# Opening order of a quantised macaron block: first transfers, tables and down units reordered, and weight stores issued from another queue

## The chip, the cores and the metric

The kernel runs on one core of a Trainium2 chip. The metric is the device time of one execution in microseconds (us), lower is better. Times of before: 858.51, 859.09 and 859.96 us in three runs, median 859.09.

## The reference

The input is 2048 tokens of 512 float32 features (two sequences of 1024). Three stages follow each other, each on a layer norm of the running sum:

```python
x = x + 0.5 * ffn(layernorm(x))        # gate, up, down with 4-bit weights, 512 -> 1376 -> 512
x = x + attention(layernorm(x))        # one head of width 128
x = x + 0.5 * ffn(layernorm(x))        # the same weights again
# ffn: W[k,n] = scales[g_idx[k],n] * (w4[k,n] - (z4[g_idx[k],n] + 1)) for gate, up and down
#      h = silu(x @ Wg) * (x @ Wu);  out = h @ Wd
```

Eight 4-bit values are packed in an int32; scales and zeros come per group of 128 rows, and which group a row uses is itself an input (`g_idx`).

## The kernel before, in words

**Tiling.** The inner dimension of 1376 is cut into 11 tiles (`NT`), the last 96 wide. The 2048 tokens make four pairs of 512-row halves. "Pair 0" is the first 1024 rows of the first feed-forward stage; while it works on its top half (`plain_top`), the weights are dequantised tile by tile, split into a high and a low float32r part and kept for all later pairs. Every product is three passes (`PASSES`: high-high, high-low, low-high).

**Units.** Gate, up and down of one tile are three *units*: 33 in all. `unit(u)` (L334) gives `(u % 3, u // 3)`, so the order is gate 0, up 0, down 0, gate 1, and so on. One unit passes through these steps, each on its own engine:

1. SyncE's queue loads the packed values, each packed row eight times, in `load_units` (L484 to L503), into one of six slots: four issues for a gate or up unit, one for a down unit. From unit 6 on it waits until the unit that had the slot is unpacked.
2. VectorE shifts and masks (`unpack`, L1681).
3. TensorE multiplies a one-hot matrix by a table of zeros and one of scales (`scales_zeros`, L789; bf16, L811 for gate and up, L808 for down): these spread the groups over the rows, into PSUM banks 2 and 3. It waits for the unit before to be dequantised (`s_wf`).
4. VectorE subtracts the zeros and multiplies by the scales (`dequantise`, L1691; the product into `wf` is L1705). `wf` has two slots, so the product of unit u waits until the low part of unit u-2 is made and until the float32 store of unit u-2 has landed (`d_full`, L1704).
5. ScalarE copies `wf` to the high part (`w_hi`, L1255); GpSimd subtracts to get the low part (`w_lo`, L2096).
6. SyncE's queue stores the float32 values of gate and up units to `wfull` (`save_full`, L519, issue L523); a later phase reads them back.

**What sets the order.** All of it is written by hand: each engine has a program of its own, and semaphores join them. SyncE's queue is strictly in order: in the loop at L583, `save_full(u)` comes ahead of `load_units([u + 6])`, the row loads and the saves of finished tiles (`save_plain`, L514), so a store waits behind the issues ahead of it.

**The opening.** SyncE issues the gate and up scales, their zeros, the group numbers, identity and shifts, then unit 0 (L563 to L571). ScalarE's queue issues the four row tiles of x (256 KB each) and the gate and up group indices, GpSimd's the down scales, zeros and indices. GpSimd cuts each scale into three bf16 parts (`cut_scales`, five steps), VectorE unpacks the zeros (`unpack_zeros`), and `table` (L401) sends these to the table tiles: the up table by SyncE, the gate table by ScalarE, in both cases after all five cuts and the zeros. VectorE computes the layer-norm statistics (L1615 to L1625), GpSimd the power -0.5 (L2088), ScalarE applies it (L1245), TensorE transposes the rows (L1020). The one-hots take a clamp, a compare and a second compare (`clamp`, `compare_low`, `one_hot`): for gate and up on VectorE, for the 768 down columns on GpSimd with the last step on VectorE. `keep_warm(n)` (L732) issues n dummy matmuls of 128x128.

**TensorE's tile loop** (L815) is: gate product i, table products of a unit to come, up product i, table products, down product i-1, table products. It runs `keep_warm(6)` after up 0, and before the loop `keep_warm(10)`, `(6)`, `(6)`.

Of the kernel before, what the change touches and what calls it, by code (L numbers as in the profile page):

```python
# [7 lines left out]
F32 = mybir.dt.float32  # L8
# [64 lines left out]
def macaron(nc, x, w_qkv, b_qkv, w_o, b_o, packed, scales, zeros, g_idx, ident, shifts, groups, out):  # L73
    ctx = ExitStack()
    with ctx:
# [52 lines left out]
        spare = place("spare", [P, 1], F32)  # L128
        mx = place("mx", [P, QT], F32)
# [115 lines left out]
        def sem(name):  # L245
# [3 lines left out]
        d_small, d_grp, d_cut_gu, d_cut_d, d_idx_gu, d_idx_d, d_bqkv, d_wq, d_wo, d_bo = (  # L249
            sem(n) for n in ("d_small", "d_grp", "d_cut_gu", "d_cut_d", "d_idx_gu", "d_idx_d", "d_bqkv", "d_wq", "d_wo", "d_bo"))  # L250
# [82 lines left out]

        def unit(u):  # L334
            return u % 3, u // 3
# [17 lines left out]
        for n in range(UNITS):  # L353
            q_count[n % QSLOTS] += 16 * (1 if n % 3 == 2 else KT)
            q_ready.append(q_count[n % QSLOTS])
# [11 lines left out]
        def full_saves(u):  # L367

            return 16 * len([v for v in range(u % 2, u, 2) if v % 3 < 2])
# [31 lines left out]
        def table(eng, m, at_row=0):  # L401
# [6 lines left out]
            for j in range(3):  # L408
                eng.dma_start(dst[at_row + j * g:at_row + (j + 1) * g, :], parts[:, j, :]).then_inc(done, 16)
            row = at_row + Z_ROW  # L410
            eng.dma_start(dst[row:row + g, :], zb.rearrange("p c j -> p (c j)")).then_inc(done, 16)
# [39 lines left out]
        GU_COLS, DOWN_COLS = slice(0, HID), slice(HID, HID + D_COLS)  # L451

# [4 lines left out]
        def out_bank(b, j):  # L457
            return PT_BANK + j % 2 if by_dve(b, j) else OUT_BANK

# [3 lines left out]
        def _(sp):  # L463
# [20 lines left out]
            def load_units(units):  # L484
                for u in units:
                    if u >= UNITS:
                        return
                    m, i = unit(u)
                    s = u % QSLOTS
                    if u >= QSLOTS:  # L490

                        sp.wait_ge(s_int, u - QSLOTS + 1)
                    for k in range(1 if m == 2 else KT):

                        if m == 2:
                            rows = packed[2][i * 16:i * 16 + width(i) // PACK, :]
                            dst = qs[:, s, :, :].rearrange("p k c -> p (k c)")[0:width(i), :]
                        else:
                            rows = packed[m][k * 16:(k + 1) * 16, i * P:i * P + width(i)]
                            dst = qs[:, s, k, 0:width(i)]  # L500
                        n_rows, n_cols = rows.shape
                        src = rows.rearrange("r (o c) -> r o c", o=1).to_broadcast([n_rows, PACK, n_cols])
                        sp.dma_start(dst, src).then_inc(d_q[s], 16)  # L503

# [9 lines left out]
            def save_plain(i):  # L514
                sp.wait_ge(s_wlo, 3 * i + 2)
                sp.dma_start(kept(i, slice(P1, P2 + 1)), as_kept(i, plain(i)[:, 0:2, :, :, :])).then_inc(d_kept[i], 16)
                sp.dma_start(kept(i, slice(P3, P3 + 1)), as_kept(i, plain(i)[:, 3:4, :, :, :])).then_inc(d_kept[i], 16)

            def save_full(u):  # L519
                m, i = unit(u)  # L520
                if m < 2:
                    sp.wait_ge(s_wf, u + 1)
                    sp.dma_start(unit_view(u, wfull[i, :, m, :]), unit_view(u, wf[:, u % 2, :])).then_inc(d_full[u % 2], 16)  # L523
# [40 lines left out]
            for m in range(2):  # L564
                sp.dma_start(sc_gu[:, m * SC:(m + 1) * SC], flat(scales[m], SC)).then_inc(d_cut_gu, 16)
            for m in range(2):
                sp.dma_start(zq_gu[m * ZP:(m + 1) * ZP, :], flat(zeros[m], ZC)).then_inc(d_cut_gu, 16)
            sp.dma_start(grp[:, :], groups).then_inc(d_grp, 16)
            sp.dma_start(idt[:, :], ident).then_inc(d_small, 16)
            sp.dma_start(shift[:, :], shifts).then_inc(d_small, 16)  # L570
            load_units([0])  # L571

            sp.wait_ge(s_cut, CUT_STEPS)
            sp.wait_ge(s_tab, ZERO_STEPS)
            table(sp, 1)
            load_units([1, 2])
            sp.wait_ge(s_cut, 2 * CUT_STEPS)
            sp.wait_ge(s_tab, 2 * ZERO_STEPS)
            table(sp, 2)
            load_units([3, 4, 5])  # L580


            for u in range(UNITS):  # L583
                save_full(u)
                load_units([u + QSLOTS])
                if u == 3:
                    load_rows(1, x, ROWS)
# [4 lines left out]
                if u >= 4 and u % 3 == 1:  # L592
                    save_plain(u // 3 - 1)
# [49 lines left out]
            sp.dma_start(wo_raw[:, :], w_o).then_inc(d_wo, 16)  # L643
# [72 lines left out]
        def _(pe):  # L716
# [72 lines left out]
            def scales_zeros(u):  # L789
# [4 lines left out]
                w = width(i)  # L794
                if u:
                    if u in (2, 3 * D_TILES + 2):

                        if u == 2:
                            pe.wait_ge(s_oh, 4)
                        pe.wait_ge(d_tab[2 if u == 2 else 3], 64)  # L800

                    pe.wait_ge(s_wf, u)
                g = (GK, GK, GD)[m]
                row = FOLD if m == 1 or (m == 2 and i >= D_TILES) else 0
                for rows, bank in ((slice(row + Z_ROW, row + Z_ROW + g), Z_BANK), (slice(row, row + 3 * g), S_BANK)):
                    if m == 2:
                        col = i * P - (D_FROM if row else 0)
                        mm = pe.matmul(ps[0:w, bank, :], oh_d[rows, col:col + w], tab_d[rows, :], start=True, stop=True)  # L808
                    else:
                        for k in range(KT):  # L810
# [4 lines left out]
            def plain_top():  # L815

                for i in range(NT):
                    pe.wait_ge(s_wlo, 3 * i + 1)
# [3 lines left out]
                    if i == 0:  # L822

                        plain_product(0, 0, 0, by_tile=True)
                        scales_zeros(2)
# [1412 lines left out]
```

## Time and profile before

| what | us |
|---|---|
| median of three runs (lowest to highest) | 859.09 (858.51 to 859.96) |
| the profiled execution | 858.8 |
| its span, first to last instruction | 857.0 |
| TensorE busy in the span | 832.5 |
| VectorE / ScalarE / GpSimd busy | 479.6 / 271.1 / 243.1 |

PE is TensorE, PEld its weight loads, DVE VectorE, ACT ScalarE, POOL GpSimd, SP SyncE; a q behind a name is that engine's instruction queue, which also issues DMAs. Times in a timeline are from the span's start. A bracket behind a row says how long the engine was idle before it and whose event ended that. Matmuls are pipelined, so a busy TensorE is not TensorE at its peak, and dummy matmuls count as busy.

### The profile page before, as it was taken

The page shows a single profiled execution, that of the slowest core. Times are in us where ns is not written, and L with a number is a line of the kernel's source. Part 1 is how long each engine was busy: PE and PEld are TensorE (multiplying, and loading weights), DVE is VectorE, ACT ScalarE, POOL GpSimd, SP SyncE. Part 2 cuts the span into 40 slices and gives each one's busy share as a digit, 9 for nine tenths or more (in the row PEclk, how much of TensorE's full clock was granted, in tenths as well). Part 3 has the DMA queues.
Part 4 walks back from the last instruction along what each step waited for, and adds up shares of the span by engine and source line. Part 5 has one row for each costly group of instructions (what it writes and reads, how often), then busy time and mean ns, then how long its engine had stood idle before and what let it go on. Part 6 is the DMA issues. An engine that isn't in the chain of part 4 may idle for free.

```text
span 857.0 us, 10735 instructions
## 1 busy us (share of the span) xinstructions
PE 832.5 (97%) x4040; PEld 677.3 (79%) x4040; DVE 479.6 (56%) x800; ACT 271.1 (32%) x465; POOL 243.1 (28%) x197
## 2 busy tenths in 40 slices
PE   4799999999999999999999999999999999999998
PEld 4477678887888888788888888888887888888786
DVE  5577763564745463455877686545445744444452
ACT  3233222253511211242565783112212511112121
POOL 6344431463200524030225453151510201101100
PEclk9999999999999999999999999999999999999999
DMA  5667647895485444241215237844444064444121
GB/s 135 203 202 245 216 172 229 306 338 200 166 329 171 129 167 123 77 160 67 82 55 169 71 130 259 324 149 157 139 136 164 36 212 145 153 154 148 40 98 50
DMA packets 72271, 139.36 MB, mean 163 GB/s; under 512 B 25548, under 2 KB 36476, under 8 KB 67228
## 3 DMA queue, kind: packets, MB, share of 16 engines
q1 hardware_dynamic: 70908, 136.91, 47.5%
q10 hardware_dynamic: 1152, 1.36, 0.6%
q8 instruction: 32, 0.52, 0.3%
q0 software_dynamic: 160, 0.42, 0.2%
q14 instruction: 19, 0.16, 0.1%
HBM read 100.54 MB, written 37.95 MB: 162 GB/s over the span
## 4 chain that ended last, share of the span: by engine, by line
PE 73%; DVE 1%; ACT 1%; issue 0%; POOL 0%; DVEq 0%; ACTq 0%; POOLq 0%
PE ps L722 37%; PE ps L729 34%; PE ps L740 2%; PE ps L1125 1%; DVE pT L1604 0%; ACT pr L1464 0%; POOL t L2083 0%; ACT oT L1240 0%; PE ps L1051 0%; DVE oT L1604 0%; DVE t L1604 0%; DVE hT L1604 0%; DVE mx L1920 0%; ACT xn L1245 0%; DVE u L1607 0%
## 5 line engine op out<-in xcount | busy, mean ns | idle before, releaser
L722 PE MATMUL ps<-blk,ring 128*128 128x512 f32 (+1 forms) x1386 | 320.9, 389 | 0.1
L722 PEld LDWEIGHTS ps<-blk,ring 128*128 128x128 f32 (+1 forms) x1386 | 256.7, 185 | 58.1 <-DVE blk L1604 0.5
L729 PE MATMUL ps<-wd,hT 128*128 128x512 f32 (+1 forms) x1056 | 250.7, 392 | 0.8 <-DVE hT L1604 0.7
L729 PEld LDWEIGHTS ps<-wd,hT 128*128 128x128 f32 (+1 forms) x1056 | 196.8, 188 | 43.4 <-DVE hT L1604 1.2
L2125 POOL TENSOR_TENSOR h<-h,u 128x512 f32<-128x512 f32 (+1 forms) x33 | 42.7, 1295 | 324.2 <-ACT h L1359 324.2
L729 PE MATMUL ps<-xT,wp 128*128 128x512 f32 x480 | 115.7, 395 | 0.9 <-POOL wp L2083 0.7
L729 PEld LDWEIGHTS ps<-xT,wp 128*128 128x128 f32 x480 | 88.4, 188 | 22.4 <-issue 2.0
L1607 DVE TENSOR_TENSOR u<-ps,p1s 128x512 f32<-128x512 f32 (+1 forms) x66 | 45.4, 687 | 97.3 <-PE ps L722 97.2
L1359 ACT ACTIVATE h<-h 128x512 f32<-128x512 f32 (+1 forms) x33 | 20.9, 632 | 176.1 <-DVE h L1607 176.1
L1607 DVE TENSOR_TENSOR u<-ps,u 128x512 f32<-128x512 f32 (+1 forms) x66 | 45.6, 691 | 25.6 <-PE ps L722 24.6
L1607 DVE TENSOR_TENSOR h<-ps,p1s 128x512 f32<-128x512 f32 (+1 forms) x33 | 22.8, 691 | 64.1 <-PE ps L722 64.1
L1604 DVE TENSOR_TENSOR hT<-h,hT 128x512 fp32r<-128x512 f32 (+1 forms) x44 | 30.7, 712 | 24.8 <-ACT hT L1240 24.8
L1354 ACT ACTIVATE g<-ps 128x512 f32<-128x512 f32 (+1 forms) x33 | 19.7, 598 | 76.0 <-PE ps L722 76.0
L1240 ACT ACTIVATE hT<-u 128x512 fp32r<-128x512 f32 (+1 forms) x33 | 20.9, 632 | 64.5 <-DVE u L1811 64.5
L1811 DVE TENSOR_TENSOR u<-u,g 128x512 f32<-128x512 f32 (+1 forms) x33 | 38.8, 1177 | 1.1
L2093 POOL TENSOR_SCALAR xn<-xn,mv,rstd 128x512 f32<-128x512 f32 x18 | 38.3, 2139 | 0.5
L1240 ACT ACTIVATE hT<-h 128x512 fp32r<-128x512 f32 (+1 forms) x44 | 27.0, 629 | 35.5 <-PE ps L729 35.5
L2083 POOL TENSOR_TENSOR wp<-wf,wp 128x512 fp32r<-128x512 f32 x20 | 26.7, 1333 | 39.3 <-ACT wp L1240 39.3
L1604 DVE TENSOR_TENSOR hT<-u,hT 128x512 fp32r<-128x512 f32 (+1 forms) x33 | 22.8, 692 | 23.1 <-ACT hT L1240 23.1
L2088 POOL TENSOR_TENSOR rstd<-rstd,mhalf 128x4 f32<-128x4 f32 x12 | 14.9, 1244 | 69.5 <-DVE rstd L1625 69.5
L1836 DVE SCALAR_TENSOR_TENSOR xres<-ps,xres 128x512 f32<-128x512 f32 x32 | 21.6, 689 | 18.7 <-PE ps L729 18.5
L1604 DVE TENSOR_TENSOR wi<-qs,ps 128x512 bf16<-128x512 int32 (+2 forms) x33 | 22.3, 676 | 16.9 <-PE ps L811 12.0
(124 smaller groups left out, 877.7 us busy)
## 6 DMA issues: line engine op xcount, KB each, us to landing
ring<-wsaved SPq DMA_DIRECT2D x29, 1024.0 KB, 5.1
ring<-wsaved SPq DMA_DIRECT2D x33, 768.0 KB, 4.4
wsaved<-wp SPq DMA_DIRECT2D x10, 1024.0 KB, 4.5
stream<-xres SPq DMA_DIRECT2D x32, 256.0 KB, 2.3
xn<-stream SPq DMA_DIRECT2D x8, 1024.0 KB, 6.7
xres<-stream SPq DMA_DIRECT2D x32, 256.0 KB, 4.0
wfull<-wf SPq DMA_DIRECT2D x20, 256.0 KB, 2.8
wsaved<-wp SPq DMA_DIRECT2D x10, 512.0 KB, 3.0
```

The lines of the kernel that those rows point to most:

```text
L722: mm = pe.matmul(ps[0:w, bank, :], ring[:, slot, which, a, kt, 0:w], blk[:, which, b, kt, :], start=not onto and kt == 0 and n == 0, stop= ...
L729: mm = pe.matmul(bank_ap, lhs(a), rhs(b), start=first and n == 0, stop=last and n == 2)
L1240: return act.activation(dst, src, ACT.Copy)
L1354: act.activation(g1[0:w, n % 2, :], ps[0:w, product_bank(n // NT + 1, 0), :], ACT.Silu).then_inc(s_g1, 1)
L1359: act.activation(hidden(i)[0:width(i), :], hidden(i)[0:width(i), :], ACT.Silu).then_inc(s_g2, 1)
L1604: return dve.tensor_tensor(out=dst, in0=a, in1=b, op=ALU.subtract)
L1607: return dve.tensor_tensor(out=dst, in0=a, in1=b, op=ALU.add)
L1811: dve.tensor_tensor(out=u2[0:w, n % 2, :], in0=u2[0:w, n % 2, :], in1=g1[0:w, n % 2, :], op=ALU.mult)\
L1836: dve.scalar_tensor_tensor(out=xres[:, r, :], in0=ps[:, down_bank(q, half, r), :], scalar=0.5, in1=xres[:, r, :], op0=ALU.mult, op1=ALU.ad ...
L2083: return pool.tensor_tensor(out=dst, in0=a, in1=b, op=ALU.subtract)
L2093: pool.tensor_scalar(x_rows(t)[:, r, :], x_rows(t)[:, r, :], mv[:, t % 2, r, 0:1], rstd[:, t % 2, r:r + 1], ALU.subtract, ALU.mult).then_i ...
L2125: pool.tensor_tensor(out=hidden(i)[0:w, :], in0=hidden(i)[0:w, :], in1=u3[0:w, n % 2, :], op=ALU.mult).then_inc(s_h2, 1)
```

## The change

- **Unit order.** Gate 0, up 0, then for each tile gate i, up i, down i-1, and the last down at the end. `made(m, i)` gives a unit's place; waits that had `3 * i + n` use it.
- **First transfers.** On SyncE the group numbers move ahead of the zeros; the zeros get semaphores of their own (`d_zq_gu`, `d_zq_d`). ScalarE's queue takes the down zeros ahead of x, and units 0 and 1 after the indices. GpSimd's index loads move behind the first cut.
- **Tables.** SyncE sends all gate and up pieces, each as soon as it is cut; ScalarE sends none.
- **ScalarE** runs one Silu on a spare column early, and issues the float32 store of a gate or up unit itself, right behind its copy of it. It applies the layer norm of the second 512 rows, which VectorE did.
- **One-hots of down.** The first 128 columns are made first; GpSimd makes its part of the other 640 ahead of the low parts of units 3 and 4, VectorE its part in tile 1.
- **TensorE.** Table products of unit 0 come ahead of the row transposes, those of unit 1 between the second and third row tile, those of unit 2 ahead of gate 0. `keep_warm` is 4 and 4 ahead of the loop (10, 6, 6 before) and 2 after up 0 (6 before).
- Smaller: one semaphore for two attention weights instead of two, later places of `deviation(1)` and of the second rows' statistics.

```diff
+        UNIT_ORDER = ((0, 0), (1, 0)) + tuple(mi for i in range(1, NT) for mi in ((0, i), (1, i), (2, i - 1))) + ((2, NT - 1),)
         def unit(u):
-            return u % 3, u // 3
+            return UNIT_ORDER[u]
+        def made(m, i):
+            return UNIT_ORDER.index((m, i)) + 1
...
@@ sync
+            sp.dma_start(grp[:, :], groups).then_inc(d_grp, 16)
             for m in range(2):
-                sp.dma_start(zq_gu[...], flat(zeros[m], ZC)).then_inc(d_cut_gu, 16)
-            sp.dma_start(grp[:, :], groups).then_inc(d_grp, 16)
+                sp.dma_start(zq_gu[...], flat(zeros[m], ZC)).then_inc(d_zq_gu, 16)
...
-            load_units([0])
-            sp.wait_ge(s_cut, CUT_STEPS)
-            sp.wait_ge(s_tab, ZERO_STEPS)
-            table(sp, 1)
-            load_units([1, 2])
+            for j in range(3):
+                sp.wait_ge(s_cut, 2 * j + 1)
+                for m in range(2):
+                    table(sp, m, pieces=(j,))
+            sp.wait_ge(s_tab, 2 * ZERO_STEPS)
+            for m in range(2):
+                table(sp, m, pieces=(3,))
+            load_units(sp, [2, 3])
             sp.wait_ge(s_cut, 2 * CUT_STEPS)
-            sp.wait_ge(s_tab, 2 * ZERO_STEPS)
             table(sp, 2)
-            load_units([3, 4, 5])
+            load_units(sp, [4, 5])
             for u in range(UNITS):
-                save_full(u)
-                load_units([u + QSLOTS])
-                if u == 3:
+                load_units(sp, [u + QSLOTS])
+                if u == 5:
                     load_rows(1, x, ROWS)
...
@@ tensor, plain_top
                     plain_product(0, 0, 0, by_tile=True)
-                    scales_zeros(2)
...
                     scales_zeros(3)
                     plain_product(0, 0, 1, (2, 3))
-                    scales_zeros(4)
-                    keep_warm(6)
+                    keep_warm(2)
...
@@ tensor, opening
-            keep_warm(10)
+            keep_warm(4)
+            pe.wait_ge(d_tab[0], 64)
+            pe.wait_ge(s_oh, 3)
+            scales_zeros(0)
             for r in range(RT):
+                if r == 2:
+                    pe.wait_ge(d_tab[1], 64)
+                    scales_zeros(1)
                 pe.wait_ge(s_ln[0], r + 1)
...
-            scales_zeros(0)
-            keep_warm(6)
-            pe.wait_ge(d_tab[1], 64)
-            scales_zeros(1)
-            keep_warm(6)
+            scales_zeros(2)
+            keep_warm(4)
             plain_top()
...
@@ scalar
                 copy(unit_weights(u, 0), unit_view(u, wf[:, u % 2, :])).then_inc(s_whi, 1)
+                m, i = unit(u)
+                if m < 2:
+                    act.dma_start(unit_view(u, wfull[i, :, m, :]), unit_view(u, wf[:, u % 2, :])).then_inc(d_full[u % 2], 16)
...
+            act.dma_start(cuts[1][4], flat(zeros[2], ZC_D)).then_inc(d_zq_d, 16)
             for r in range(RT):
                 act.dma_start(xn0[:, 0, r, :], x[r * P:(r + 1) * P, :]).then_inc(d_x0[r], 16)
...
-            act.wait_ge(s_cut, CUT_STEPS)
-            act.wait_ge(s_tab, ZERO_STEPS)
-            table(act, 0)
+            act.wait_ge(s_cst, 1)
+            act.activation(spare_act[:, :], mhalf[:, 0:1], ACT.Silu)
+            load_units(act, [0, 1])
             ln_apply(0)
+            w_hi(0)
             rows_hi(0)
-            w_hi(0)
...
@@ vector
-            dve.wait_ge(d_cut_gu, 64)
+            dve.wait_ge(d_zq_d, 16)
+            unpack_zeros(dve, tables, *cuts[1])
+            ln_stats(0, (0, 1))
+            dve.wait_ge(d_zq_gu, 32)
             unpack_zeros(dve, tables, *cuts[0])
-            ln_stats(0)
+            ln_stats(0, (2, 3))
             ln_var(0)
...
             unpack(0)
-            dve.wait_ge(d_cut_d, 32)
-            unpack_zeros(dve, tables, *cuts[1])
-            dequantise(0, unpack_next=False)
+            dequantise(0)
+            dequantise(1, unpack_next=False)
             rows_lo(0)
-            unpack(1)
+            unpack(2)
...
@@ gpsimd
-            pool.wait_ge(d_cut_gu, 64)
+            pool.wait_ge(d_cut_gu, 32)
             cut_scales(pool, cutter, *cuts[0])
+            for row, first in ((0, 0), (FOLD, D_FROM)):
+                pool.dma_start(idx[...], spread(g_idx[2][first:first + D_COLS])).then_inc(d_idx_d, 16)
...
-            clamp(pool, hots, DOWN_COLS, GD)
-            compare_low(pool, hots, DOWN_COLS, 1, oh_d[:, :])
+            clamp(pool, hots, DOWN_FIRST, GD)
+            compare_low(pool, hots, DOWN_FIRST, 1, oh_d[:, 0:P])
             for u in range(UNITS):
-                if u == 16:
+                if u == 3:
+                    clamp(pool, hots, DOWN_REST, GD)
+                if u == 4:
+                    compare_low(pool, hots, DOWN_REST, 1, oh_d[:, P:D_COLS])
+                if u == 19:
                     deviation(1)
                 w_lo(u)
```

## Rows read from the trace of the kernel before

**Rows 1.** The page: the span and TensorE's busy time

```profile
span 857.0 us, 10735 instructions
PE 832.5 (97%) x4040; PEld 677.3 (79%) x4040; DVE 479.6 (56%) x800; ACT 271.1 (32%) x465; POOL 243.1 (28%) x197
```

**Rows 2.** Windows: stretch, length, busy us (instructions) by engine, granted clock, DMA share, GB/s

```profile
0.00:10.70 10.70, 0.00 (x1) 0.00 (x1) 4.53 (x20) 0.00 (x0) 6.07 (x20) 1.00 0.82 199
10.70:21.14 10.44, 10.21 (x76) 9.49 (x77) 7.87 (x20) 6.91 (x10) 6.88 (x4) 1.00 0.36 72
21.14:46.86 25.72, 19.50 (x110) 13.34 (x110) 16.28 (x28) 7.95 (x12) 8.74 (x7) 1.00 0.70 218
46.86:139.52 92.66, 91.79 (x499) 66.80 (x497) 63.17 (x112) 28.54 (x47) 34.42 (x27) 1.00 0.64 208
```

**Rows 3.** Waits of TensorE, whole span: total us, times, longest

```profile
PE ps L811 <- DVE wf L1705: 6.0, 7, 1.9
```

**Rows 4.** Timeline of TensorE, 21 to 47 us: start, length, line, operation, [idle before]

```profile
21.14 3.01 PE L729 MATMUL ps<-xT,wp 128*128 128x512 f32 x12
24.61 0.39 PE L808 MATMUL ps<-tab_d,oh_d 10*128 10x512 bf16 x2 [0.46 <-DVE oh_d L448]
...
28.97 0.41 PE L811 MATMUL ps<-tab_gu,oh_gu 4*128 4x128 bf16 x8 [1.58 <-DVE wf L1705]
...
43.27 0.40 PE L811 MATMUL ps<-tab_gu,oh_gu 4*128 4x128 bf16 x8 [1.93 <-DVE wf L1705]
43.60 3.01 PE L729 MATMUL ps<-wd,hT 128*128 128x512 f32 x12
...
46.86 1.43 PE L729 MATMUL ps<-xT,wp 128*128 128x512 f32 x5
```

**Rows 5.** Timeline of VectorE and SyncE's queue, 24 to 43 us: stores and waits for them

```profile
24.51 1.52 SPq L523 DMA_DIRECT2D wfull<-wf  x1
...
28.23 0.69 DVE L1705 TENSOR_TENSOR wf<-wi,ps 128x512 f32<-128x512 bf16 x1 [2.40 <-DMA wfull<-wf]
...
42.52 0.69 DVE L1705 TENSOR_TENSOR wf<-wi,ps 128x512 f32<-128x512 bf16 x1 [3.31 <-DMA wfull<-wf]
```

**Rows 6.** The stores of line L523, to 140 us: issue to landing

```profile
DMA to landing us min/median/max: 2.0/2.7/6.2
```

**Rows 7.** Timeline of all engines, 3 to 20 us: the opening

```profile
3.24 0.61 ACTq L1432 DMA_DIRECT2D idx<-in_L_ffn_up_g_idx  x1
...
4.00 2.59 SPq L503 DMA_DIRECT2D qs<-in_L_ffn_gate_qweight  x4
...
7.50 2.88 ACTq L409 DMA_DIRECT2D tab_gu<-parts_gu  x3
...
10.57 0.43 DVE L442 TENSOR_SCALAR idf<-idx 128x512 f32<-128x512 int32 x1 [0.49 <-DMA idx<-in_L_ffn_up_g_idx]
...
10.70 4.64 PE L736 MATMUL ps<-idt 128*128 128x128 f32 x20 [10.70 <-DMA shift<-in_shifts]
...
11.18 1.28 ACT L1245 ACT_TABLE_LOAD   x1 [11.18 <-issue]
11.36 2.83 POOL L442 TENSOR_SCALAR idf<-idx 128x768 f32<-128x768 int32 x1
...
12.16 0.74 DVE L448 SCALAR_TENSOR_TENSOR oh_gu<-idf,grp,oh_gu 128x512 bf16<-128x512 f32 x1
12.48 2.93 ACT L1245 ACTIVATE xn<-xn,nmr,rstd 128x512 f32<-128x512 f32 x4
12.94 0.49 DVE L1688 TENSOR_SCALAR qs<-qs,shift 128x512 int32<-128x512 int32 x1
...
17.37 1.60 PE L736 MATMUL ps<-idt 128*128 128x128 f32 x12
17.59 0.69 DVE L1604 TENSOR_TENSOR wi<-qs,ps 128x512 bf16<-128x512 int32 x1 [2.34 <-PE ps L811]
...
18.92 2.48 DVE L1604 TENSOR_TENSOR xT<-ps,xT 128x512 fp32r<-128x512 f32 x4
```

## What the change should do, predicted before it was run

> **What bounds the kernel now.** I read the page first: TensorE is busy for 832.5 of 857.0 us [rows 1], so 24.5 us at most are idle time, and only what shortens TensorE's work or its waits counts. The windows say where the idle time lies [rows 2]: 10.7 us before the first matmul, 6.22 (25.72 less 19.50) between the first gate product at 21.14 and the third at 46.86, and 0.87 (92.66 less 91.79) in the rest of pair 0's top half. In the stretch from 10.70 to 21.14 TensorE looks busy, but much of that is dummy matmuls. So the case is decided in the first 47 us. The list of waits then names the cause [rows 3]: 6.0 us in 7 waits of the gate and up table products (L811) for VectorE's dequantised unit (L1705). The timeline gives the pieces [rows 4]: 1.58 us before 28.97, 1.93 before 43.27, also 0.46 for the down one-hot at 24.61. One level below, VectorE itself waits for a float32 store to land, 2.40 us and 3.31 us [rows 5]. The first of these stores was issued only at 24.51, because SyncE's queue put other issues ahead of it. From 46.86 on TensorE is nearly full, so time won before that point moves everything behind it.
>
> The profiled execution took 858.8 us, 0.3 below the median of 859.09; the sum is made against it and 0.3 is added at the end. Outside its span lie 1.8 us.
>
> **Part 1, the head.** Today VectorE waits 2.34 us before 17.59 because unit 0's table products stand behind the transposes [rows 7]. In the new order they need the tables and the one-hot, which ends at 12.90 (12.16 and 0.74). Unpacking unit 0 takes to about 13.4 (0.49), with the table products beside it. VectorE then does unit 0 (subtraction 0.69, product the same length), unpacks unit 1 (0.49), and does unit 1 (1.4): about 16.9. The table products of unit 1 stand between the second and third row tile and need unit 0, done at 14.9; the rows come from ScalarE, whose four steps end at about 15.4 [rows 7], so this blocks little. TensorE then does unit 2's table products (0.39, as in [rows 4]) and four dummies (1.60 for six, so 1.07 [rows 7]): 18.4. The low parts of the rows (2.48 for four) follow on VectorE from 16.9; the first is there at 17.5, and each of the rest sooner than TensorE needs it. So gate 0 starts at 18.4 rather than 21.14.
>
> Two things can delay that. *ScalarE's issues:* it now issues the down zeros, x, the indices, a table load and units 0 and 1 before it applies the norm. Before, its indices end at 3.85; with one more issue and the load (1.28) it is at 5.6. Eight issues cost 5.2 us at SyncE's price (2.59 for four) or 7.7 at the price that ScalarE paid for table pieces (2.88 for three), ending at 10.8 or 13.3 [rows 7]. The norm starts at 12.48, so the cost is 0 to 0.8 us, and as much again where unit 1's data lands after VectorE wants it. I take 0.3. *The other end:* the group indices, for which VectorE waits at 10.57, might land earlier since fewer bytes compete, which gains up to 0.5; I take nothing. Head: 18.7, a gain of **2.4**, bounds 0.9 to 3.2. The early cuts, the table pieces on SyncE and the moved index loads are costed at nothing: the one-hot's end at 12.90 covers them. Without that cover each SyncE issue is 0.65.
>
> **Part 2, waits from gate 0 to gate 2.** The 6.22 us are the pool. The store moves to ScalarE, right behind the copy: the one issued at 24.51 would go at about 16, those after it up to 5 us sooner. The down one-hot is cut to 128 of 768 columns for the first use, and down 0 comes after gate 1. Following all five engines from 18.7 in the new order, TensorE meets one wait of some 0.3 (unit 5's table products behind VectorE's unit 4). GpSimd's clamp of the other 640 columns (5/6 of 2.83 [rows 7], 2.4 us) stands ahead of unit 3's low part; that ends about 1.5 us before up 1 needs it, so it costs nothing, and up to 2.4 if that cover is gone. Gain **5.9**, before the next item.
>
> **Stores that still land late.** A store took 2.0 to 6.2 us to land, median 2.7 [rows 6], and the 3.31 us wait is for one that fell together with a row load of 1 MB. Tile products come every 3.26 us (43.60 to 46.86 [rows 4]), so two units are 6.5 apart. Take off the product (0.69), ScalarE's copy (about as long) and the next unit's subtraction (0.69): about 4.4 us are free. VectorE has another 1.1 (3.0 less 0.69, 0.69 and 0.49) in each product before TensorE notices, so a store may take 5.5 us from its issue. The DMA engines' share was 0.70 in this stretch [rows 2] and rises when it gets shorter, so two or three stores will be later than that. Cost **1.0**, bounds 0 to 4. The page "DMA: Bandwidth & Descriptors" of the Trainium skill (Issuing engines are not separate DMA queues) says that DMAs from any engine run on the same 16 DMA engines, so another issuer saves only the time to initiate. By that rule the move cures late issue and no slow landing; the trace agrees in so far as the store behind the 3.31 us wait had been issued long before it landed.
>
> **Part 3, TensorE's own work.** Four dummies fewer after up 0: **1.07**. Unit 2's table products move ahead of gate 0 (counted there) and out of this stretch: **0.39**. ScalarE's reload of the Silu table goes, but nothing waited there: 0.
>
> **Part 4, the rest of the top half.** VectorE loses the norm of the second rows, ScalarE gets it. ScalarE is busy 28.54 of 92.66 us [rows 2]; 22 store issues at the 0.6 us of an index issue [rows 7] add 13 us over the whole top half, which fits, but each stands ahead of the next copy. Of the 0.87 us still idle I take back **0.6**, bounds -1 (a loss) and 0.87. The late down units have their place: at the end TensorE has transposes and a down product between the last up product and the last down product. 0.
>
> **Clock.** The granted clock is 1.00 throughout [rows 2], which is the 2.4 GHz level. But the first ten dummies took 4.64 us, 0.46 each, and later ones 0.27 [rows 7]: the first work runs near the 1.2 GHz level. With 4 rather than 10 dummies some of the transposes and table products will run slowly. Most of that is hidden behind VectorE until 16.9; what shows is the four dummies and gate 0, 4.1 us if both run at half speed. I take a loss of **0.5**, since TensorE has work almost without a pause from 13 on; bounds 0 and 4.1.
>
> **Sum:** 2.4 + 5.9 - 1.0 + 1.07 + 0.39 + 0.6 - 0.5 = 8.9. So 858.8 - 8.9 + 0.3 = 850.2 us.
>
> **Rivals.**
>
> *A, the clock stays low into the first tile.* For it: 0.46 against 0.27 us, and only four dummies. Against it: after waits of 1.58 and 1.93 us the six- and twelve-matmul groups kept their pace [rows 4]. It costs the other 3.6 of the bound: 853.8. The page "TensorE: Matmul & The Clock Gate" (Part 4: PE-mode transpose) holds that transposes do not count as busy for the clock in the same way, which speaks for this case, since transposes now take the place of dummies. Chance 0.10.
>
> *B, the transfers become the bound.* The DMA engines were busy 0.70 of 25.72 us, 18.0 us [rows 2]; I shorten the stretch to some 18.3. If nearly all of it has to pass, the stretch takes about 20, and later stores and loads collide: 2 to 5 us given back, 852 to 855. For it: 3.31 us of waiting in the fullest moment [rows 5]. Against it: six slots lie ahead, and half of the row load falls later. Chance 0.17.
>
> *C, no difference.* The head is bound elsewhere (indices, norm), gate 0 stays at 21.1, and the stores land as late as before, so Part 2 is lost as well: 858. Chance 0.05.
>
> *D, slower.* The stores on ScalarE's queue land late every time. The price is the time over 5.5 us, in each of the 20 stores that a later unit waits for. The 8.9 us are gone at 0.45 us each, a landing of 5.95. At 6.2 on each, the longest of before, it is 0.7 x 20 = 14 us: 864. That maximum speaks for it, the median of 2.7 strongly against it [rows 6]. Chance 0.06.
>
> **How the numbers follow.** The forecast (847 to 852) has 0.62, A 0.10, B 0.17, C 0.05, D 0.06. The range goes from 847.0 (head and rest at their best, no late stores) to 854.5, which takes in A and most of B. A measurement of this kernel tells about 0.2% (1.7 us) from no change. Faster by more: 0.62 + 0.10 + 0.17 = 0.89; within: 0.05; slower: 0.06.
>
> **What would show it.** Right: gate 0's first product near 18.7, gate 2's near 38.6 (46.86 less the 8.3 of the head, Parts 2 and 3, stores and clock) instead of 46.86; the waits for L1705 on TensorE fall from 6.0 to under 2 us; store issues on ScalarE's queue right behind each copy, VectorE's waits for them under 2 us in all; first matmuls at 0.46 us but gate 0 in about 3 us. Wrong: gate 0 in 5 us or more (A); DMA share near 1 from 19 to 40 us with unpacking waiting for packed values (B); gate 0 at 21 (C); the same wait for a store before every second product down to 130 us (D). If ScalarE's norm starts after 13.3, the issue price was too low.

## The result and the profile after

The changed kernel takes 855.25 us (853.05 to 856.65 in seven runs) against 859.09; the ratio is 0.995, 95% interval 0.9934 to 0.9967. It is faster, by 3.8 us, less than half of the 8.9 that were predicted (850.2, range 847.0 to 854.5). The profiled execution took 854.81 us, 4.0 below that of before.

In the profile after, line numbers are a little higher: L729 is now L736 (products), L811 is L816 and L808 is L814 (table products), L736 is L743 (dummies), L1020 is L1030 (row transposes), L1705 is L1720, L523 is L1268. The page of the kernel after:

```profile
span 853.0 us, 10668 instructions
PE 829.8 (97%) x4004; PEld 674.2 (79%) x4004; DVE 481.9 (56%) x798; ACT 272.3 (32%) x469; POOL 243.8 (29%) x198
```

Its windows, in the stretches of [rows 2]:

```profile
0.00:10.70 10.70, 1.37 (x6) 1.38 (x7) 6.11 (x30) 1.49 (x2) 6.15 (x19) 1.00 0.85 198
10.70:21.14 10.44, 4.28 (x31) 3.26 (x30) 3.76 (x8) 3.56 (x5) 2.81 (x4) 1.00 0.53 104
21.14:46.86 25.72, 25.05 (x140) 18.65 (x139) 21.66 (x33) 9.20 (x16) 14.56 (x10) 1.00 0.77 239
46.86:139.52 92.66, 92.66 (x495) 66.95 (x494) 62.84 (x110) 31.32 (x51) 33.68 (x26) 1.00 0.64 210
```

The third and fourth rows are what was hoped for: TensorE is idle for 0.67 us where it was idle for 6.22, and not at all later. The second row is the loss: TensorE works for 4.28 of 10.44 us. Its timeline from 9 to 43 us shows why:

```profile
9.33 2.08 PE L743 MATMUL ps<-idt 128*128 128x128 f32 x8 [9.33 <-DMA shift<-in_shifts]
17.56 0.61 PE L816 MATMUL ps<-tab_gu,oh_gu 4*128 4x128 bf16 x8 [6.16 <-DMA tab_gu<-zb_gu]
18.10 1.97 PE L1030 MATMUL ps<-idt,xn 128*128 128x128 f32 x8
20.00 0.61 PE L816 MATMUL ps<-tab_gu,oh_gu 4*128 4x128 bf16 x8
20.54 1.97 PE L1030 MATMUL ps<-idt,xn 128*128 128x128 f32 x8
22.44 0.61 PE L816 MATMUL ps<-tab_gu,oh_gu 4*128 4x128 bf16 x8
22.98 2.01 PE L743 MATMUL ps<-idt 128*128 128x128 f32 x8
24.71 4.41 PE L736 MATMUL ps<-xT,wp 128*128 128x512 f32 x18
...
42.08 0.39 PE L814 MATMUL ps<-tab_d,oh_d 10*128 10x512 bf16 x2 [0.67 <-DVE wf L1720]
42.40 3.02 PE L736 MATMUL ps<-xT,wp 128*128 128x512 f32 x12
```

Gate 0 starts at 24.71, where it was 21.14 [rows 4]; gate 2 at 42.40, where it was 46.86. TensorE waits 6.16 us for the gate table. The other engines and queues in the opening of the kernel after:

```profile
4.00 6.17 SPq L418 DMA_DIRECT2D tab_gu<-parts_gu  x6
...
7.18 2.61 ACTq L490 DMA_DIRECT2D qs<-in_L_ffn_up_qweight  x4
...
10.22 3.25 SPq L421 DMA_DIRECT2D tab_gu<-zb_gu  x2
...
11.53 0.74 DVE L458 SCALAR_TENSOR_TENSOR oh_gu<-idf,grp,oh_gu 128x512 bf16<-128x512 f32 x1
11.65 2.92 ACT L1250 ACTIVATE xn<-xn,nmr,rstd 128x512 f32<-128x512 f32 x4 [5.67 <-DVE nmr L1644]
...
15.68 0.49 DVE L1703 TENSOR_SCALAR qs<-qs,shift 128x512 int32<-128x512 int32 x1 [3.40 <-DMA qs<-in_L_ffn_gate_qweight]
```

The one-hot ends at 12.27 and the norm starts at 11.65, both sooner than in [rows 7]. But unit 0 is there only at 15.68 and the table at 17.56. Transfers, not engines, hold the start. Their issue took longer too: SyncE's eight table issues run from 4.00 to 13.47, two of them 2.4 and 2.6 us long, where the prediction had 0.65 for each.

The profiled executions of all kernels fit one rule. What lies behind the start of gate 0 is nearly the same length in every kernel that has the new order, 827.4 to 828.8 us; in the kernel before it is 835.9. So the change has two halves: **7.6 us won behind gate 0, 3.6 us lost ahead of it.** These are single executions; the seven runs of the kernel after spread over 3.6 us themselves.

| kernel | table products of unit 0 | gate 0 | span less gate 0 | ratio to before, interval |
|---|---|---|---|---|
| before | 17.03 | 21.14 | 835.86 | |
| after | 17.56 | 24.71 | 828.29 | 0.9950 (0.9934 to 0.9967) |
| e1 unit 1 late | 15.30 | 21.16 | 827.84 | 0.9909 (0.9892 to 0.9925) |
| e2 zeros by ScalarE | 17.66 | 23.61 | 828.59 | 0.9930 (0.9915 to 0.9945) |
| e3 22 dummies | 16.80 | 22.07 | 828.83 | 0.9936 (0.9914 to 0.9958) |
| e4 stores only | 16.33 | 20.45 | 831.75 | 0.9938 (0.9921 to 0.9955) |
| e5 old transfers | 15.25 | 21.11 | 827.69 | 0.9914 (0.9894 to 0.9934) |
| e6 the same, 10 dummies | 16.70 | 21.97 | 828.03 | 0.9898 (0.9880 to 0.9916) |
| e7 down indices early | 18.61 | 25.76 | 828.64 | 0.9942 (0.9925 to 0.9959) |
| e8 pieces late | 16.43 | 23.31 | 827.69 | 0.9919 (0.9900 to 0.9938) |
| e9 tables by two queues | 15.04 | 21.99 | 827.41 | 0.9908 (0.9895 to 0.9922) |
| e10 pieces and unit 1 late | 15.35 | 20.62 | 828.28 | 0.9925 (0.9912 to 0.9939) |
| e11 unit 2 early | 19.17 | 26.17 | 828.23 | 0.9969 (0.9957 to 0.9981) |
| e12 no unit early | 15.80 | 23.64 | 828.26 | 0.9922 (0.9908 to 0.9935) |
| e13 as e10, indices last | 13.72 | 22.38 | 828.62 | 0.9939 (0.9925 to 0.9952) |
| e14 as e9, indices last | 14.33 | 21.10 | 828.60 | 0.9914 (0.9900 to 0.9929) |

The times in columns two to four come from one execution each, and the opening varies between executions (the shifts, for which the first dummy waits, land between 7.8 and 12.9 us); the ratios come from several. In before, e3, e4, e10 and e13 TensorE was busy with other work until the time in the second column, so there it is only an upper bound of the landing. How much one execution is worth is seen where the transfers are the same: the table was there at 15.25 in e5 and at 16.70 in e6, at 17.56 in the kernel after and by 16.80 in e3. Differences of up to about 1.5 us in the second column mean nothing alone; that the units delay the tables rests on the ratios below.

### The profile page after: what moved, and what is told of

Read it like the earlier page. It is cut to its first block, busy times and chain, and to the rows that moved or that the text cites. A ratio compares the mean times of both kernels' runs of the same rounds, so it can differ in the third digit from the quotient of the medians.

```text
span 853.0 us, 10668 instructions
## 1 busy us (share of the span) xinstructions
PE 829.8 (97%) x4004; PEld 674.2 (79%) x4004; DVE 481.9 (56%) x798; ACT 272.3 (32%) x469; POOL 243.8 (29%) x198
## 4 chain that ended last, share of the span: by engine, by line
PE 73%; DVE 2%; ACT 1%; issue 0%; POOL 0%; DVEq 0%; ACTq 0%; POOLq 0%
PE ps L729 37%; PE ps L736 33%; PE ps L747 2%; PE ps L1130 1%; DVE xn L1651 1%; DVE pT L1619 0%; ACT pr L1479 0%; POOL t L2109 0%; ACT oT L1245 0%; DVE oT L1619 0%; DVE t L1619 0%; DVE hT L1619 0%; PE ps L1056 0%; DVE mx L1946 0%; ACT xn L1250 0%
## 5 line engine op out<-in xcount | busy, mean ns | idle before, releaser
L729 PE MATMUL ps<-blk,ring 128*128 128x512 f32 (+1 forms) x1386 | 320.9, 389 | 0.1
L729 PEld LDWEIGHTS ps<-blk,ring 128*128 128x128 f32 (+1 forms) x1386 | 256.7, 185 | 58.1 <-DVE blk L1619 0.5
L736 PE MATMUL ps<-wd,hT 128*128 128x512 f32 (+1 forms) x1056 | 251.1, 392 | 0.9 <-DVE hT L1619 0.8
L736 PEld LDWEIGHTS ps<-wd,hT 128*128 128x128 f32 (+1 forms) x1056 | 196.8, 188 | 43.8 <-DVE hT L1619 1.2
L736 PE MATMUL ps<-xT,wp 128*128 128x512 f32 x480 | 115.8, 396 | 0.0
L736 PEld LDWEIGHTS ps<-xT,wp 128*128 128x128 f32 x480 | 88.5, 188 | 21.2 <-issue 2.0
```

What stands on the lines that cost most here:

```text
L729: mm = pe.matmul(ps[0:w, bank, :], ring[:, slot, which, a, kt, 0:w], blk[:, which, b, kt, :], start=not onto and kt == 0 and n == 0, stop= ...
L736: mm = pe.matmul(bank_ap, lhs(a), rhs(b), start=first and n == 0, stop=last and n == 2)
```

## The experiments

**The second half alone (e4).** The kernel before, with only the store moved:

```diff
-                save_full(u)                    # SyncE's loop
+                act.dma_start(unit_view(u, wfull[i, :, m, :]), unit_view(u, wf[:, u % 2, :])).then_inc(d_full[u % 2], 16)   # in w_hi
```

> Kernel before, with nothing changed but the issue of the float32 stores: ScalarE issues each behind its copy of the unit, SyncE issues none. Theory of the prediction (late issue of stores is most of the 6.2 us that TensorE waits between gate 0 and gate 2): gate 0 stays at 21.1, the waits of VectorE for stores fall from 7.8 to under 2.5 us, gain 3 to 4.5 us, so 855. If the order of units and the smaller one-hot are what counts, the gain is 2 us or less.

(At the end of its loop SyncE waits for the last stores, which ScalarE now issues.) VectorE's waits for stores in the first 140 us, before and in this run, and then two products of TensorE in this run:

```profile
DVE wf L1705 <- DMA wfull<-wf: 7.8, 6, 3.3
```

```profile
DVE wf L1709 <- DMA wfull<-wf: 0.2, 1, 0.2
```

```profile
20.45 3.06 PE L730 MATMUL ps<-xT,wp 128*128 128x512 f32 x12
...
41.66 3.04 PE L730 MATMUL ps<-xT,wp 128*128 128x512 f32 x12
```

The waits for stores go from 7.8 to 0.2 us, and gate 0 to gate 2 takes 21.21 us instead of 25.72. One edit gives 4.1 of the 7.6 us behind gate 0, and alone it is at least as fast as the whole change (its ratio means 5.3 us, more than the 3 to 4.5 expected; the profiled gate 0 was also 0.7 sooner). The other 3.5 us belong to the order of units, the smaller one-hot and the dummies together; they were not separated.

**What holds the tables: less ahead of them (e1, e12), more ahead of them (e11).**

```diff
-            load_units(act, [0, 1])     # e1: act [0], sp [1, 2, 3]; e12: sp [0, 1, 2, 3]; e11: act [0, 1, 2], sp [3]
-            load_units(sp, [2, 3])
```

> Kernel after, with unit 1 issued by SyncE behind the table pieces rather than by ScalarE ahead of them (four issues, 256 KB less in the way of the tables). Theory T (the zero pieces of the gate and up tables land late, at 17.5 us, because the transfers of units 0 and 1 keep the DMA engines and SyncE's issues full): zero pieces land 2 to 3.5 us sooner, gate 0 starts near 22 instead of 24.7, time about 2.5 us under the kernel after, near 852.5. Rival C (TensorE's low clock from 17.6 to 24.7 is what makes gate 0 late): gate 0 moves by less than 1 us. Rival I (unit 1's data then lands too late): gate 0 waits for unit 1's unpacking instead, no gain.

> The suspected cost taken away: the kernel after with no unit ahead of the tables; SyncE issues units 0 to 3 behind the zero pieces, at about 9.5 us. Theory T: tables land by 12.5 to 13 and SyncE's piece issues take 0.6 to 0.8 us each; then unit 0, issued last, is what VectorE waits for (15 us), gate 0 near 21, time as with unit 1 alone held back (852.5). If tables land at 16 or later even so, the units are not the cause.

> The suspected cost increased: the kernel after with unit 2 as well issued by ScalarE ahead of the tables (256 KB more, 512-byte rows). Theory T: zero pieces land 2 to 3 us later still, near 20, gate 0 near 27, time 2 to 3 us over the kernel after (857.5 to 859), of which up to 0.8 us can come from ScalarE's norm behind four more issues. If the transfers are not what the tables wait for, no change beyond that 0.8.

TensorE in e1, e12 and e11, in this order:

```profile
15.30 0.60 PE L816 MATMUL ps<-tab_gu,oh_gu 4*128 4x128 bf16 x8 [5.44 <-DMA tab_gu<-zb_gu]
```

```profile
15.80 0.60 PE L816 MATMUL ps<-tab_gu,oh_gu 4*128 4x128 bf16 x8 [5.88 <-DMA tab_gu<-zb_gu]
```

```profile
19.17 0.61 PE L816 MATMUL ps<-tab_gu,oh_gu 4*128 4x128 bf16 x8 [8.84 <-DMA tab_gu<-zb_gu]
```

256 KB less ahead of the tables: 2.3 us sooner, and the ratio falls clear of that of the kernel after, by 0.0041 or 3.5 us. 256 KB more: 1.6 us later and a gain smaller by 1.6 us, where 2 to 3 were expected, with an interval that overlaps that of the kernel after. So the units' transfers do delay the tables, which e1 shows; e11 only points the same way. But with none ahead (e12) the tables are no sooner than with one, at 15.80 rather than the 12.5 to 13 expected: a second cause holds them until about 15. The time of e12 is the one it foresaw (852.5, measured 852.75), for the reason that was written down: the unit lands last there (16.86, where VectorE unpacks it).

**Does the place in a queue matter (e2)?**

```diff
+            act.wait_ge(s_tab, 2 * ZERO_STEPS)
+            for m in range(2):
+                table(act, m, pieces=(3,))      # between load_units(act, [0]) and load_units(act, [1])
```

> Kernel after, with the two zero pieces issued by ScalarE between units 0 and 1, SyncE issuing only the scale pieces ahead of units 2 and 3. Theory T: the zero pieces are issued at about 7.5 us instead of 10.2 to 12.8, ahead of unit 1; they land by 13 to 14, gate 0 starts near 21.5, time 3 us under the kernel after. If only the fullness of the DMA engines counts and not the place in a queue, they land no sooner than 16 and the gain is under 1 us.

ScalarE's queue, then TensorE, then VectorE in e2:

```profile
7.25 1.50 ACTq L421 DMA_DIRECT2D tab_gu<-zb_gu  x2
```

```profile
17.66 0.61 PE L814 MATMUL ps<-tab_gu,oh_gu 4*128 4x128 bf16 x8 [7.55 <-DMA tab_gu<-zb_gu]
```

```profile
16.95 0.59 DVE L1705 TENSOR_SCALAR qs<-qs,shift 128x512 int32<-128x512 int32 x1 [5.63 <-DMA qs<-in_L_ffn_gate_qweight]
```

The zero pieces went out 3 to 5 us sooner than in the kernel after, and the tables were no sooner. Unit 0, issued at 4.6 to 7.2, landed at 16.95. The expectation of 13 to 14 fell, and the landing came out as in the branch that only the fullness counts; the gain over the kernel after, 0.0020 or 1.7 us, is above the 1 us of that branch, with overlapping intervals. The edit is not clean, though: SyncE, without the zero pieces to wait for, issued unit 2 from 8.34 instead of 13.51, so more bytes were under way at the same time. Place in a queue and fullness are not fully separated.

**Early pieces and early indices (e8, e7).**

```diff
-            for j in range(3):
-                sp.wait_ge(s_cut, 2 * j + 1)
+            sp.wait_ge(s_cut, CUT_STEPS)        # e8: hold all pieces until every cut and the zeros are done
+            sp.wait_ge(s_tab, 2 * ZERO_STEPS)
```

> Kernel after, with the table pieces held back until all five cuts and the zeros are done (as before), still all on SyncE. If sending each piece as soon as it is cut brings anything, this is 1 us or more slower than the kernel after. Theory T (the pieces only wait in the full DMA engines): zero pieces land at 17 to 18 as in the kernel after, time within 1 us of it.

> Kernel after, with only the two down index loads (384 KB) put back ahead of the first cut on GpSimd's queue. If their late place makes them collide with units 0 and 1 and the tables, the zero pieces land 1 to 2 us sooner and the time falls by as much; if only the sum of the bytes in flight counts, they then delay x and the gain is 0 or a loss of up to 1 us.

Held back, the pieces landed at 16.43 instead of 17.56, which alone is within what executions differ by, and the ratio is 0.9919: sending each as soon as it is cut brings nothing, and probably costs (the intervals of the two only just meet), which neither branch had foreseen. The place of the down indices (e7) makes no difference that can be told.

**The old transfers with the new order, and the clock (e5, e6, e3).** e5 puts units, tables and down indices back as they were among the first transfers (group numbers and down zeros stay early); e6 is e5 with `keep_warm(10)`, e3 the kernel after with `keep_warm(22)`, each in place of the first `keep_warm(4)`.

> Kernel after, with the first transfers as before (unit 0 and then the up table and units 1 to 3 by SyncE, the gate table by ScalarE after all cuts, the down indices early); the order of the work on TensorE, VectorE and the store issues stay as in the kernel after. Theory T (transfers decide; in the kernel before the tables were there by 13 us): table products of unit 0 start near 13.5 instead of 17.6, gate 0 near 19 to 20.5 instead of 24.7, time 4 to 5.5 us under the kernel after, near 851. If the new order of the engines itself is what makes gate 0 late, gate 0 stays at 23 or later.

> The run above with 10 dummy matmuls at the start instead of 4. Clock as a second cause: 1 to 2 us less than the run above, since the transposes and the products around them run at full rate. If the clock rises by itself in time, no difference.

> Kernel after, with 22 dummy matmuls instead of 4 at the start, so that TensorE works until about 17 us. Rival C (clock): table products and transposes run at 0.4 and 1.0 us instead of 0.61 and 1.97, gate 0 starts 2 to 2.5 us sooner, near 22.5, time 2 to 2.5 us under the kernel after. Theory T alone: the records get shorter but gate 0 still waits for VectorE's chain from the table products on; gain 1 us or less.

TensorE in e5, then in e6, then in e3:

```profile
15.25 0.60 PE L813 MATMUL ps<-tab_gu,oh_gu 4*128 4x128 bf16 x8 [2.10 <-DMA tab_gu<-zb_gu]
...
21.11 4.36 PE L733 MATMUL ps<-xT,wp 128*128 128x512 f32 x18
```

```profile
16.70 0.40 PE L813 MATMUL ps<-tab_gu,oh_gu 4*128 4x128 bf16 x8 [0.42 <-DMA tab_gu<-zb_gu]
```

```profile
10.09 6.77 PE L743 MATMUL ps<-idt 128*128 128x128 f32 x44 [10.09 <-DMA shift<-in_shifts]
16.80 0.40 PE L816 MATMUL ps<-tab_gu,oh_gu 4*128 4x128 bf16 x8
17.12 1.09 PE L1030 MATMUL ps<-idt,xn 128*128 128x128 f32 x8
...
22.07 4.37 PE L736 MATMUL ps<-xT,wp 128*128 128x512 f32 x18
```

With the old transfers the tables land 2.3 us (e5) or 0.9 us (e6) sooner than in the kernel after, later than the 13.5 expected. What the new transfer order costs is better read from the ratios, in two pairs with few and with many dummies: 0.9914 (e5) against 0.9950, and 0.9898 (e6) against 0.9936 (e3), 3.1 and 3.3 us. The intervals of each pair only just touch or overlap a little; that of e6, which also has more dummies, is clear of the kernel after.

With TensorE kept at work, the table products take 0.40 us and eight transpose records 1.09, against 0.61 and 1.97 in the kernel after. From the table products to gate 0 it takes 5.27 us (e3, e6 and e10 alike) against 7.15. In the runs the dummies brought 0.0014 (e3) and 0.0016 (e6), some 1.3 us each, with overlapping intervals: two results that agree, neither clear alone, and for e3 between what its two branches foresaw. e6 has the lowest ratio of all, 0.9898, but its interval overlaps those of e1, e5, e9 and e14 among others, so it is one of several near 0.99 rather than the best.

**Putting the gains together (e9, e10), and the floor (e13, e14).** e9: unit 0 by SyncE at 4 us, up table by SyncE and gate table by ScalarE, 12 dummies. e10: e8 and e1 together, 14 dummies. e13 and e14 are e10 and e9 with 11 dummies and

```diff
             deviation(0)
+            for row, first in ((0, 0), (FOLD, D_FROM)):
+                pool.dma_start(idx[...], spread(g_idx[2][first:first + D_COLS])).then_inc(d_idx_d, 16)
             hots = maker(pool, s_ohd)
```

> Meant as the best version: the kernel after with unit 0 issued by SyncE at 4 us, each table sent whole by one queue (up by SyncE, gate by ScalarE) after the cuts and zeros, units 1 to 3 behind, down indices late as in the kernel after, and 12 dummy matmuls at the start. Rule found so far: the time is the start of gate 0 plus 828 us of span. Theory T: tables land by 14, gate 0 starts near 19.5 to 21, time 848.5 to 851. If the late indices help nothing, it equals the run with the old transfers and 10 dummies (851.4).

> The kernel after with the two edits that each brought some 3 us put together: table pieces held until all cuts and zeros are done, unit 1 issued by SyncE behind them; and 14 dummies. If the two act on the same full stretch, they bring little more together than one: gate 0 near 21, 851 to 852. If they add up, gate 0 near 19, 849.

> The kernel with pieces and unit 1 late, 11 dummies instead of 14, and the two down index loads (384 KB) issued by GpSimd only behind the power of the norm, at about 10 us, behind every table piece's data. If they are what keeps the tables from landing before 15 us, the tables land at 13 or 13.5, gate 0 starts near 18.5 to 19, time 847 to 849. If the floor of 15 belongs to the table pieces themselves (many 86-byte rows), the tables land at 15 as before, gate 0 at 20.5 to 22, 851 to 852.5.

> The kernel with unit 0 by SyncE and each table whole by one queue, 11 dummies instead of 12, with the same late down index loads. Same question with the pieces issued by two queues at once, by 10 us: with the index loads as the cause, tables at 12.5 to 13 and gate 0 near 18, 846.5 to 848.5; with the pieces themselves as the cause, tables at 15, gate 0 at 20.5 to 22, 850.5 to 852.

e9 missed: its tables came at 15.04 and not by 14, gate 0 at 21.99, and its time is that of e6, so the late index loads brought nothing there that can be told. The gains of e1 and e8 do not add up (e10: 0.9925), as in the branch that both relieve the same stretch. But in e10 the fourteen dummies ran until 15.35 and the gate table was there by then, so the dummies may have cost some of the gain; a run with fewer was not made.

In e13, SyncE's queue, the down index loads on GpSimd's, TensorE, and the window from 8 to 12 us (its last two numbers are DMA share and GB/s):

```profile
9.66 0.67 SPq L421 DMA_DIRECT2D tab_gu<-zb_gu  x1
...
12.13 0.66 SPq L421 DMA_DIRECT2D tab_gu<-zb_gu  x1
```

```profile
10.72 1.14 POOL L2174 DMA_DIRECT2D idx<-in_L_ffn_down_g_idx  x2
```

```profile
13.72 0.61 PE L813 MATMUL ps<-tab_gu,oh_gu 4*128 4x128 bf16 x8
14.26 1.30 PE L1027 MATMUL ps<-idt,xn 128*128 128x128 f32 x8
17.39 0.40 PE L813 MATMUL ps<-tab_gu,oh_gu 4*128 4x128 bf16 x8 [1.83 <-DMA tab_gu<-zb_gu]
```

```profile
8.00:12.00 4.00, 1.00 0.19 35
```

The answer lies between the two expectations: the gate table is there by 13.72 (e13) and at 14.33 (e14), the earliest of all runs, so the index loads may have held it for about a microsecond; e14 and e9 differ by only 0.7, less than two executions of the same transfers do. For the up table e13 does not ask the question: the index loads were issued at 10.72, ahead of its last piece (12.13 to 12.79). TensorE could start on it only at 17.39, with a DMA share of 0.56 between 12 and 17.

A table piece has no fixed landing time. From the end of the issue of the gate table's zero piece to its use it is 2.6 us in e8, 3.0 in e1 and in e5, at most 3.4 in e13, 4.8 in the kernel after and 6.8 in e12: the early ones mostly just take longer. What holds an early piece (its short source rows, its four long target rows, a few engines out of the 16 that are still full, or other loads under way) the mean share can't tell, and was not tried; the cause of the floor stays open. Neither e13 nor e14 became faster: the index loads now fall on unit 1 (VectorE waits 2.27 us for it in e13, 0.61 in e14) and TensorE's clock drops.

The clock drops visibly in e9, where twelve dummies ended at 12.7 and TensorE then waited for the table. Windows of e9; the third number is the granted clock:

```profile
12.00:16.00 4.00, 0.87 0.51 116
16.00:20.00 4.00, 0.50 0.51 149
```

0.50 is the 1.2 GHz level. From table products to gate 0 e9 took 6.95 us, so that what the tables won was lost again. The page "TensorE: Matmul & The Clock Gate" of the Trainium skill (Part 4: PE-mode transpose) says that transposes do not count as busy in the same way. In e9 and in the kernel after the low level lasts through the transposes, which agrees with it. In e1, e2 and e5 it does not: there TensorE ran nothing but table products and transposes after its wait, and the second eight transpose records already got faster (1.72, 1.80 and 1.63 us instead of 1.97), with 0.40 for the table products behind them. In e1:

```profile
18.27 1.72 PE L1030 MATMUL ps<-idt,xn 128*128 128x128 f32 x8
19.93 0.40 PE L816 MATMUL ps<-tab_gu,oh_gu 4*128 4x128 bf16 x8
```

So transposes do not keep the level low by themselves here; no run separates them from the table products and gaps between them.

## Why the prediction was wrong

**Part 1, the head: this step failed.** It said that "the early cuts, the table pieces on SyncE and the moved index loads are costed at nothing: the one-hot's end at 12.90 covers them". The one-hot ended at 12.27, but the table came at 17.56. The prediction had no row for the landing of the tables. In the kernel before, TensorE comes to its table products only after the transposes, at 17.03 and without a wait, so the trace bounded the landing from above by 17, not by 13. The same trace did show how long other loads of the opening took, from issue to landing (last number, us):

```profile
idx<-in_L_ffn_up_g_idx ACTq DMA_DIRECT2D x1, 128.0 KB, 7.2
sc_gu<-in_L_ffn_gate_scales SPq DMA_DIRECT2D x1, 21.5 KB, 2.6
```

The last of eight issues of 0.65 from 4.0 starts at 8.6; with 2.6 to 7.2 from there, an estimate from these rows puts the tables at 11 to 16, a term and a range that the sum did not have. e1, e6 and e12 show what the step left out: units issued ahead of the tables delay them, with 256 KB less worth 3.5 us of the whole, and something not yet found holds the gate table until 14 to 15 even without them (13.72 is the earliest, in e13). The working from there on was right: it gave 5.4 us from the table products (13.0) to gate 0 (18.4), and e3, e6 and e10 measure 5.27. Of the 6.0 us by which gate 0 is later than the 18.7 forecast, some 4.7 are the table (17.56 instead of 12.90) and 1.4 the clock.

**Clock.** A loss of 0.5 was taken, bounds 0 to 4.1; measured are 7.15 less 5.27, 1.9 us in the profiled executions and about 1.3 in the runs. The reason given, that TensorE "has work almost without a pause from 13 on", fell with Part 1: it stood idle from 11.4 to 17.56. Gate 0 itself ran at full rate (18 records, the last six of them up 0's, in 4.41 us; twelve take 3.01 in [rows 4]), so rival A had the mechanism but not the place.

**Parts 2 to 4 were right in their sum and a little small.** They summed to 7.0 with late stores charged (5.9 - 1.0 + 1.07 + 0.39 + 0.6), measured 7.6; of the single terms only the stores were measured alone (e4, 4.1). TensorE's waits for L1720 are down to one; the store landing in the kernel after, for [rows 6]:

```profile
DMA to landing us min/median/max: 2.1/3.3/4.8
```

No store was later than 5.5 us, so the 1.0 was not paid, VectorE never waits for one in the kernel after, and rival D did not come. The page "DMA: Bandwidth & Descriptors" of the Trainium skill (Issuing engines are not separate DMA queues) says that another issuer saves only the time to initiate a DMA. The trace agrees in so far as the landing got no shorter: its median went from 2.7 to 3.3, while the first store went out at 19.73 instead of 24.51. ScalarE's issues cost 0.65 each, SyncE's price, and the norm started at 11.65, before the 13.3 that would have told of the higher price.

**The rivals.** The outcome is half of B and half of C, which I had not paired: transfers did become the bound, as in B, but ahead of gate 0, not between 19 and 40 us; and gate 0 stayed at 21 or later, as in C, which I had tied to the loss of Part 2 without a reason. A rival "head late, rest won" would have read 858.8 - 7.0 + 0.3 = 852 with gate 0 at 21.1, and with one more term for a later gate 0 the 855 that came.

**Two bounds do not follow from their terms.** Head: 18.4 with both delays at their largest (0.8 and 0.8) leaves a gain of 1.1, not 0.9. Range: the head at 3.2, Part 4 at 0.87, no late stores and no loss to the clock give 847.6, not 847.0. Neither changes how the prediction came out.

## What to carry to other kernels

Where an engine reaches its operand late for another reason, the trace says nothing of when the operand landed but that it was before that; take that time as the upper bound, and put its distance in the range. Moving loads earlier in an opening that is already full of transfers can delay the ones that are needed first, and issuing those from another queue did not help here (e2); count the bytes ahead of each needed piece. An engine's waits for a store that was issued late are cheap to remove: issuing the store from the engine that has just read its source gave 4 us with one moved issue.

## What was not expected of the hardware

- The granted clock reads 1.00 in the kernel after while the records are slow (table products 0.61 us against 0.40, eight transpose records 1.97 against 1.09). It shows 0.50 only after a rise and a fall, as in e9, e13 and e14: the level at the start has to be read from durations.
- ScalarE's queue issues DMAs while its activation table loads: the load runs from 4.48 for 1.28 us, and two issues of unit 0 run from 4.55 for 1.26 us. I had put the load ahead of the issues.
- A store's issue starts with ScalarE's copy, not behind it (19.73 and 19.72 in the kernel after), and takes 0.34 us as a median; SyncE's took 0.49.
